# Second experts' first layer as whole products, each tile's weights by a transfer

## The reference

```python
h = einsum('btd,edh->bteh', x, W1) + b1      # D = 128, H = 512, E = 8
y = einsum('bteh,ehd->bted', gelu(h), W2) + b2
out = einsum('bted,bte->btd', y, combine)    # two experts per token, softmax weights
x = layer_norm(x + out) * gamma + beta
```

## Time and profile before

| | us |
|---|---|
| median of 3 runs (lowest, highest) | 1482.44 (1477.04, 1482.59) |
| the profiled execution | 1481.06 |
| its span | 1479.3 |
| PE busy in the span | 1286.8 (87%) |
| DVE, ACT, POOL busy | 955.5, 858.0, 606.1 |
| DMA traffic over the span | 54.68 MB, 37 GB/s |

### The profile page before, as it was taken

How to read it: one execution, slowest core, us unless ns; L and a number is a source line. 1 busy time by engine, 2 the same in 40 slices (tenths; PEclk the granted TensorE clock), 3 DMA queues, 4 the chain that set the end, 5 groups by cost and what they waited for, 6 DMA issues and landing times.

```text
span 1479.3 us, 28486 instructions
## 1 busy us (share of the span) xinstructions
PE 1286.8 (87%) x9302; PEld 793.7 (54%) x9302; DVE 955.5 (65%) x3308; ACT 858.0 (58%) x1679; POOL 606.1 (41%) x783
## 2 busy tenths in 40 slices
PE   3867899999999999999999999899888986989982
PEld 1323445555555555555555545455555654878872
DVE  4465665667576766776676766656756663676784
ACT  3775675667566766675666576645434443455553
POOL 1000233342444425342533353335435455657674
PEclk7989899999999999999999999999989998999996
DMA  8051590000000000000000000001020001142322
GB/s 333 1 214 39 9 4 1 1 9 1 8 10 14 8 1 16 8 8 1 17 7 8 1 16 1 8 5 69 2 77 16 1 8 37 46 116 70 119 74 91
DMA packets 65455, 54.68 MB, mean 37 GB/s; under 512 B 41016, under 2 KB 51648, under 8 KB 65056
## 3 DMA queue, kind: packets, MB, share of 16 engines
q1 hardware_dynamic: 60768, 43.48, 14.7%
q0 software_dynamic: 4544, 9.38, 1.9%
HBM read 21.03 MB, written 31.81 MB: 36 GB/s over the span
## 4 chain that ended last, share of the span: by engine, by line
PE 58%; DVE 22%; ACT 9%; issue 7%; POOL 2%; POOLq 1%; DMA 0%; SPq 0%; ACTq 0%; DVEq 0%
PE scores L1744 12%; PE outs L1762 9%; PE work L1684 7%; PE outs L1888 6%; DVE scores L1238 4%; DVE ra L1231 4%; PE work L1791 4%; PE scores L1875 3%; ACT ra L953 2%; ACT a_buf L947 2%; PE scores L1713 2%; PE outs L1967 2%; DVE parts L1273 2%; PE work L1850 1%; PE work L1861 1%
## 5 line engine op out<-in xcount | busy, mean ns | idle before, releaser
L1238 DVE CUSTOM_DVE_ANT_0 scores<-scores,mask_qk 128x512 f32<-128x512 f32 (+3 forms) x512 | 238.5, 517 | 168.7 <-PE scores L1713 168.6
L786 POOL TENSOR_SCALAR_AFFINE_SELECT big<-big 128x256 f32<-128x256 f32 x256 | 101.2, 408 | 496.4 <-ACT big L941 471.9
L941 ACT ACTIVATE big<-scores 128x1024 f32<-128x1024 f32 (+1 forms) x192 | 169.6, 884 | 231.6 <-PE scores L1744 231.5
L947 ACT ACTIVATE a_buf<-scores 128x1024 f32<-128x1024 f32 x256 | 248.7, 1029 | 47.2 <-PE scores L1875 47.0
L1744 PE MATMUL scores<-ra 64*128 64x512 f32 (+3 forms) x1536 | 187.6, 350 | 16.9 <-ACT a_buf L947 10.0
L806 POOL TENSOR_TENSOR big<-big 128x768 f32<-128x768 f32 x64 | 116.6, 1822 | 130.9 <-issue 52.9
L1762 PE MATMUL outs<-big 128*64 128x512 f32 (+3 forms) x1024 | 159.4, 455 | 0.0
L1744 PEld LDWEIGHTS scores<-ra 64*128 64x128 f32 x1536 | 123.4, 190 | 67.1 <-issue 45.7
L1888 PE MATMUL outs<-a_buf 128*16 128x512 f32 x1024 | 142.8, 632 | 2.0 <-ACT a_buf L947 2.0
L1022 ACT ACTIVATE big<-scores,b_sb 128x128 f32<-128x128 f32 x312 | 89.2, 369 | 76.4 <-PE scores L1955 76.4
L1231 DVE TENSOR_TENSOR ra<-work,ra 128x512 fp32r<-128x512 f32 x128 | 87.9, 687 | 69.7 <-ACT ra L953 69.4
(11 more groups left out here) (223 smaller groups left out, 2539.3 us busy)
## 6 DMA issues: line engine op xcount, KB each, us to landing
sorted_rows<-xrows SPq DMA_DIRECT2D x34, 520.0 KB, 6.7
qkT<-sorted_rows SPq DMA_DIRECT2D x78, 65.0 KB, 1.9
a_buf<-in_w SPq DMA_DIRECT2D x2, 2048.0 KB, 7.8
a_buf<-in_x SPq DMA_DIRECT2D x8, 256.0 KB, 2.7
x_rows<-x SPq DMA_DIRECT2D x8, 256.0 KB, 2.0
ra<-x_rows SPq DMA_DIRECT2D x8, 256.0 KB, 3.0
a_buf<-choice_rows SPq DMA_DIRECT2D x6, 256.0 KB, 4.0
yT<-choice_rows SPq DMA_DIRECT2D x5, 256.0 KB, 2.8
```

Source lines behind the costliest of these rows:

```text
L941: activation(prob1(g, i), d[:, :, 0:256] if i == 2 else d, ACT.Exp, scale=SCALE1).then_inc(unit_free("pair", g, i), 1)
L947: activation(prob0(c)[:, i * 1024:(i + 1) * 1024], unit_wait(act, "cosine", c, i), ACT.Exp).then_inc(unit_free("cosine", c, i), 1)
L1238: return v.tensor_tensor_reduce(scores_, scores_, mask_qk[:, SEQ - width:SEQ], -1.0, 3e38, ALU.add, ALU.min, neg_max[:, qt, j:j + 1])
```

## The change

The first layer is computed with the hidden channels on the partitions: the weight tile is the stationary operand, the transposed rows are the moving one, in four whole float32 products. Its result needs no transposing, so `hidden_moved` and `hidden_transposed` go, and so does the split of rows and weights into two float32r parts. The weights are no longer held whole: SP loads the 512 columns (256 KB) of each tile's expert into a ring of eight, behind the tile's rows. DVE copies the transposed rows (`x_T_moved`).

```diff
+W1_RING = 8
             def sorted_tile(n):
                 if n >= RING:
                     sp.wait_ge(y_tile_sent[n % RING], 16 * (n // RING))
                 at = sp.value_load(block_at[0:1, n:n + 1], min_val=0, max_val=BLOCKS - 1)
                 sp.dma_start(x_tile(n), sorted_rows[bass.ds(at * P, P), :]).then_inc(
                     x_tile_in[n % RING], 16)
+                if n >= W1_RING:
+                    sp.wait_ge(hidT_full, n - W1_RING + 1)
+                cols = sp.value_load(expert_at[0:1, n:n + 1], min_val=0,
+                                     max_val=(EXPERTS - 1) * HID1)
+                sp.dma_start(w1_tile(n), w1_1[:, bass.ds(cols, HID1)]).then_inc(
+                    w1_tile_in[n % W1_RING], 16)
...
-                if b == BATCH - 3:
-                    sp.wait_ge(x_taken, BATCH)
-                    sp.dma_start(w1_raw, w1_1).then_inc(w1_in, 16)
...
-            sp.wait_ge(sparse_ready, EXPERTS)
             for n in range(ALL_TILES):
...
-            def x_hi_part(n):                       # ACT
-                act.wait_ge(xt_full, n + 1)
-                if n >= 4:
-                    act.wait_ge(hid_full, n - 3)
-                copy(x2_hi[:, quarter(n)], xt_bank).then_inc(xt_hi, 1)
...
-                                      scores[:, n % 2, HID1 + c * P:HID1 + (c + 1) * P], ACT.Gelu,
+                                      scores[:, n % 2, c * P:(c + 1) * P], ACT.Gelu,
...
-                if o.i == BATCH - 1:
-                    act.wait_ge(w1_in, 16)
-                    copy(w1_hi[:, p * HID1:(p + 1) * HID1],
-                         w1_raw[:, p * HID1:(p + 1) * HID1]).then_inc(sparse_hi, 1)
...
-            def x_lo_part(n):                       # DVE
-                dve.wait_ge(xt_hi, n + 1)
+            def x_T_moved(n):
+                dve.wait_ge(xt_full, n + 1)
                 if n >= 4:
-                    dve.wait_ge(hid_full, n - 3)
-                v.tensor_tensor(x2_lo[:, quarter(n)], xt_bank, x2_hi[:, quarter(n)].bitcast(F32),
-                                ALU.subtract).then_inc(xt_lo, 1)
-            def hidden_moved(n):
-                dve.wait_ge(hid_full, n + 1)
-                if n >= 2:
-                    dve.wait_ge(hidT_full, n - 1)
-                v.tensor_copy(hid_rows(n), scores[:, n % 2, 0:HID1]).then_inc(hid_ready, 1)
+                    dve.wait_ge(hidT_full, n - 3)
+                v.tensor_copy(x_T(n), xt_bank).then_inc(xt_ready, 1)
...
-                if o.i == BATCH - 1:                # DVE
-                    dve.wait_ge(sparse_hi, p + 1)
-                    cols = slice(p * HID1, (p + 1) * HID1)
-                    v.tensor_tensor(w1_lo[:, cols], w1_raw[:, cols], w1_hi[:, cols].bitcast(F32),
-                                    ALU.subtract).then_inc(sparse_ready, 1)
...
             def hidden1(n):                         # PE
                 expert[n] = pe.value_load(expert_at[0:1, n:n + 1], min_val=0,
                                           max_val=(EXPERTS - 1) * HID1)
-                pe.wait_ge(xt_lo, n + 1)
-                if n >= 2:
-                    pe.wait_ge(hid_ready, n - 1)
-                d = scores[:, n % 2, 0:HID1]
-                cols = bass.ds(expert[n], HID1)
-                mm(d, x2_hi[:, quarter(n)], w1_hi[:, cols], start=True, stop=False)
-                mm(d, x2_hi[:, quarter(n)], w1_lo[:, cols], start=False, stop=False)
-                mm(d, x2_lo[:, quarter(n)], w1_hi[:, cols], start=False,
-                   stop=True).then_inc(hid_full, 1)
-            def hidden_transposed(n):
-                pe.wait_ge(hid_ready, n + 1)
+                pe.wait_ge(w1_tile_in[n % W1_RING], 16 * (n // W1_RING + 1))
+                pe.wait_ge(xt_ready, n + 1)
                 if n >= 2:
                     pe.wait_ge(hidT_ready, n - 1)
                 for c in range(CH1):
-                    last = nc.tensor.transpose(scores[:, n % 2, HID1 + c * P:HID1 + (c + 1) * P],
-                                               hid_rows(n)[:, c * P:(c + 1) * P], ident)
+                    last = mm(scores[:, n % 2, c * P:(c + 1) * P],
+                              w1_tile(n)[:, c * P:(c + 1) * P], x_T(n), start=True, stop=True)
                 last.then_inc(hidT_full, 1)
...
             def first_tiles():
-                pe.wait_ge(sparse_ready, EXPERTS)
+                pe.wait_ge(sparse_in, 16 * N_SPARSE)
```

More of the change, by code:

```diff
@@ L266 @@
 A0_BUF = XT_B + SEQ
-W1_HI = 0
-W1_LO = W1_HI + EXPERTS * HID1
-W2 = W1_LO + EXPERTS * HID1
+W1 = 0
+W2 = W1 + W1_RING * HID1
 B2 = W2 + EXPERTS * HID1
+X_T = B2 + EXPERTS * DIM
 Y_RING = 0
@@ L276 @@
 HID_AT = XB_RING + RING * DIM
-FINISH = HID_AT + 4 * HID1
+FINISH = HID_AT + 2 * HID1
 SPARSE = FINISH + EARLY.last * SEQ
@@ L427, in layers_kernel, with w1_tile @@
         tsum = big[:, TSUM:TSUM + 2 * 384].rearrange("p (j n) -> p j n", j=2)
-        w1_hi = a0_part(W1_HI, EXPERTS * HID1).bitcast(F32R)
-        w1_raw = a0_part(W1_LO, EXPERTS * HID1)
-        w1_lo = a0_part(W1_LO, EXPERTS * HID1).bitcast(F32R)
+        def w1_tile(n):
+            return a0_part(W1 + (n % W1_RING) * HID1, HID1)
         w2_1_sb = a0_part(W2, EXPERTS * HID1)
@@ L467, in xb_tile, with hid_T, x_T @@
             return ring(XB_RING, DIM, n)
-        def hid_rows(n):
+        def hid_T(n):
             return big[:, HID_AT + (n % 2) * HID1:HID_AT + (n % 2 + 1) * HID1]
-        def hid_T(n):
-            return big[:, HID_AT + (2 + n % 2) * HID1:HID_AT + (3 + n % 2) * HID1]
-        assert SPARSE <= BIG and B2 + EXPERTS * DIM <= A0_BUF
+        def x_T(n):
+            return a0_part(X_T + (n % 4) * P, P)
+        assert SPARSE <= BIG and X_T + 4 * P <= A0_BUF
         def quarter(n):
@@ L532, in layers_kernel @@
         kept = sem("kept")
-        w1_in = sem("w1_in")
         sparse_in = sem("sparse_in")
-        sparse_hi = sem("sparse_hi")
-        sparse_ready = sem("sparse_ready")
         sparse_step = sem("sparse_step")
@@ L539, in layers_kernel @@
         x_tile_in = [sem(f"x_tile_in{i}") for i in range(RING)]
+        w1_tile_in = [sem(f"w1_tile_in{i}") for i in range(W1_RING)]
         y_tile_sent = [sem(f"y_tile_sent{i}") for i in range(RING)]
         xt_full = sem("xt_full")
-        xt_hi = sem("xt_hi")
-        xt_lo = sem("xt_lo")
+        xt_ready = sem("xt_ready")
         xb_ready = sem("xb_ready")
-        hid_full = sem("hid_full")
-        hid_ready = sem("hid_ready")
         hidT_full = sem("hidT_full")
@@ L1078, in _ @@
                     act.wait_ge(tables_ready, 1)
-                    for n in range(3):
-                        x_hi_part(n)
                 if o.pair(-1) is not None:
@@ L1120, in _ @@
             for n in range(ALL_TILES):
-                if n + 3 < ALL_TILES:
-                    x_hi_part(n + 3)
                 if n == LATE.tile:
@@ L1531, in _ @@
                     for n in range(3):
-                        x_lo_part(n)
+                        x_T_moved(n)
                 if o.pair(-1) is not None:
@@ L1612, in scaled @@
                                 ALU.mult).then_inc(rows_ready["fin"], 1)
-            hidden_moved(0)
             for n in range(ALL_TILES + 1):
                 if n + 3 < ALL_TILES:
-                    x_lo_part(n + 3)
-                if n + 1 < ALL_TILES:
-                    hidden_moved(n + 1)
+                    x_T_moved(n + 3)
                 if n:
@@ L1931, in rows_transposed @@
                 if n >= 1:
-                    pe.wait_ge(xt_lo, n)
+                    pe.wait_ge(xt_ready, n)
                 nc.tensor.transpose(xt_bank, x_tile(n)[:, 0:DIM], ident).then_inc(xt_full, 1)
@@ L2104, in _ @@
                     hidden1(n + 1)
-                if n < ALL_TILES:
-                    hidden_transposed(n)
                 if n:
```

## The result

The changed kernel takes 1469.6 us (median of 5 runs, 1468.66 to 1473.0) against 1482.44 of the kernel before on the same chip: a ratio of 0.9914 (95% interval 0.9888 to 0.994), 12.8 us less. The forecast was 1450. The profiled execution took 1468.66 us, with a span of 1466.9 (before: 1481.06 and 1479.3).

A forecast was written before the change was run, and what follows sets the result against it. PE alone was taken to set the quiet pace, with DVE work causing stalls elsewhere and SP binding after tile 29. Gains 7 + 13.3 + 0 + 10.2 + 1 = 31.5 us from 1482.44 gave 1451, stated as 1450 (own range 1441 to 1458).

The forecast's parts named there:

- The start: Before the tile stage: PE no longer waits for rows and weights, its first product comes earlier; 7 us gained (5 to 11).
- the step i = 7: Step before the tile stage: eight DVE differences and as many ACT roundings go; 1 us gained (0 to 8).
- Tiles 29 to 77: Finishing stretch: SP's queue ends at 98 us, later than PE's 94, against 108.21 before; 10.2 us gained.
- SP and the transfers: SP's queue: a second table read and issue per tile make 2.22 us (2.0 to 2.5), more than PE's 1.89.
- PE's first layer ended by a DMA: Expected sign after tile 29 that SP binds: PE's first layer waits on SP's weights, issue pairs every 2.2 us.
- four tiles take it 9 us: POOL from tile 52: two added operations of about 1.2 us every fourth tile, 9 us against PE's 7.6.
- Tiles 1 to 25: First stretch of the tile stage: 24 tiles at 1.89 us plus 5 of stalls, 50.4 for 63.7; 13.3 us gained.
- I keep 5: Stalls between tiles 1 and 25: 5 of 12.3 us remain, for long routing chains and ACT's table change (0 to 12.3).
- PE stays near 2.1: Rival: PE's sequencer holds the tile near 2.1 us, only start and stalls gain; 1462 us, chance 0.09.
- dearer SP: Rival: SP costs 2.6 us per tile, adding 14 us after tile 29; about 1464 us, chance 0.15.
- SP free: Rival: SP does not bind and the lighter DVE leaves nearly no stall; about 1438 us, chance 0.17.
- Slower by blocked issues: Rival: SP's issues block while transfer engines are full, 1.15 us each, 3.03 per tile; 1490 us, chance 0.05.

The follow-up runs named there:

- the request made four tiles earlier: Changed kernel with SP issuing the finished rows' loads from tile 55 instead of tile 59: ratio 0.9865 to the kernel before.
- its repeat on the second chip: The changed kernel unaltered, run again as control on another chip: ratio 0.9919 to the kernel before.
- the ring of twelve: Changed kernel with twelve places for weight tiles instead of eight: ratio 0.9898 to the kernel before.
- the same ring with one read less: Changed kernel with twelve weight places and a fixed expert per tile, so SP makes no second table read: ratio 0.9861 to the kernel before.
- the two-bank kernel: Changed kernel with finished rows requested at tile 55 and two alternating PSUM banks for transposed rows: 1458.58 us on the third chip, 0.9852 to the kernel before.
- the version with weights by ACT: Changed kernel with two alternating PSUM banks, ACT issuing weights from tile 8 on, finished rows still requested at tile 59: 1453.64 us, 0.9831 to the kernel before.
- the resident one with two banks: Changed kernel with all weights loaded once, fixed expert per tile, two alternating PSUM banks for transposed rows: 1448.39 us, 0.9791 to the kernel before.
- moving the read: Changed kernel with finished rows requested at tile 55 and PE's table read placed ahead of the transpose: ratio 0.9864 to the kernel before.

## Why the prediction was wrong

**The mechanisms.** The rounded products and the transposes fell away and the product is as dear as the second layer (286 and 279 ns a record): right. The start: PE's first product moved from 1242.48 to 1234.84 us and tile 1's store by 8.64, against 8 forecast with the step i = 7. Tiles 25 to 29 took 16.60, forecast 16.6. SP needs 2.18 us for a pair, forecast 2.22, and an issue takes 0.33 (the longest of the weights' 78 took 0.75). The sign was right. The sum came out 19.1 us too high, in two terms.

**Tiles 29 to 77, 12.5 us of it: the gain that "is then 10.2, not 14".** The step that failed stands in "SP and the transfers", at "behind it stand the rows of n+1 and all later tiles, the residuals and finished rows". The finished rows were priced as ten issues of 0.47 us, never as a consumer with a due time. DVE needs the first of them at tile 52, in a stream on which the next tiles' copies depend. An SP that falls behind reaches its tile 59 too late, and 9 us are lost in one place (17.18 in place of 8.23). That this is the cause is shown by the request made four tiles earlier (DVE's wait 7.81 us in the changed kernel, 7.00 in its repeat on the second chip, 1.51 with the early request); that SP's pace makes it late, and not the ring of eight, is shown by the ring of twelve (8.33) against the same ring with one read less (2.57). The forecast that SP binds was thus right, but it showed where it wasn't looked for: "PE's first layer ended by a DMA" is not seen in the changed kernel, as the hole gives SP its lead back. Only where the hole is closed does PE wait for rows, 7.2 us in the two-bank kernel, and that SP's part in the weights costs it is shown by the version with weights by ACT, where those waits are gone.

With it failed the path of the sum: one end time for SP's whole queue (98) was set against one for PE and POOL (94), and the later was taken. SP's own part came out nearly right. The changed kernel's last weights leave at

```profile
1420.36 0.33 SPq L679 DMA_DIRECT2D a_buf<-in_w  x1
```

and with a landing of 2.9 that is 94.4 us behind tile 29's store, forecast 93.0. But from there to the last store it was to be 5.0 us and is 18.7. SP does not set the pace up to the last tile: it holds the tiles up once, at 52, and those behind the hole take 2.34 us each (53.88 / 23) at their own pace, while SP runs ahead. Where the hole is closed, SP's price is mis-sized as well: forecast 4 us (98 against 94); to tile 77 the two-bank kernel takes 108.7, 6.5 more than with the weights by ACT and 11.7 more than the resident one with two banks.

**The same stretch, POOL and a slip.** That "four tiles take it 9 us" was right for the kernels with two banks (9.27), and the 94 us for a stage without SP's limit were 3 low: the resident kernel with two banks takes 37.81 + 6.76 + 49.75 = 94.3 us to tile 76 and 2.6 more to tile 77. So even a free SP had less to give than the prediction said. Against that, the 98 us of the forecast ran to tile 77 and were compared with 108.21 to tile 76; like for like, 110.84 before, the forecast gain would have been 12.8, and the miss is 15.1 us and not 12.5.

**Tiles 1 to 25, 7.2 us of it: "I keep 5".** The quiet tile was 1.985 instead of 1.89, inside its bounds (1.80 to 2.0): 24 x 0.095 = 2.3. The stalls are 57.55 - 24 x 1.985 = 9.9 instead of 5: 4.9. They were tied to how much of DVE's time is free ("some 1.1 us of a 1.89 us tile"). DVE did get lighter (busy 31.33 of 57 us, before 48.44 of 67), and the stalls stayed, because about half of them are not load but order: one insertion in DVE's stream still delays the copy, one PSUM bank passes that on to PE, and PE's table read is queued behind. The two-bank kernel shows that the forecast's 5 us of stalls were attainable: 52.16 us, of which 4.5 are stalls, but by an edit that this change did not contain.

**The clock.** Before, PE was granted 2.4 GHz from 1249 us on; only the start of the stage was lower (0.59 in the earlier trace rows). Now the window 1328 to 1338 has 0.83, behind a stretch in which PE stood idle for 2.5 of 16 us; the hole itself has 0.63, and the 5 us behind it 0.56. No term had this. As an estimate from these grants, the 5 us behind the hole cost up to 2.2 and the 10 from 1328 up to 1.7; no run measures either by itself. Nor does idle time alone decide it. In the two-bank kernel on the third chip PE was no busier, and the grant stayed at 1.00 there and through tiles 49 to 53:

```profile
1316.00:1321.00 5.00, 3.18 (x25) 2.57 (x24) 0.78 (x3) 1.54 (x6) 4.20 (x5) 1.00 0.90 259
1321.00:1326.00 5.00, 3.28 (x28) 2.88 (x27) 2.13 (x6) 1.88 (x7) 4.29 (x7) 1.00 0.71 203
1326.00:1331.00 5.00, 5.00 (x46) 4.88 (x45) 1.95 (x7) 2.28 (x8) 4.33 (x7) 1.00 0.54 167
```

**The rivals.** The time lies beyond both near ones, 1462 (PE stays near 2.1) and 1464 (dearer SP), and for neither's reason: the quiet tile did shorten, and the pair cost 2.18, not 2.6. SP free: no. On that rival the Trainium skill, DMA: Bandwidth & Descriptors, Issuing engines are not separate DMA queues, calls the issue "usually small relative to the DMA itself"; the issue alone is (0.33 us beside a landing of 2.9), but with the table read that the address needs it is 1.09, and with the weights taken off SP tiles 29 to 76 were 6.5 us shorter. Slower by blocked issues: the weights' issues took 0.33, two of 78 more than 0.5.

What stays open: why every second quiet tile is 0.1 to 0.3 us longer than 1.89; the records put a gap ahead of its first layer at PE's own issue, and moving the read did not shorten it. Nor is it settled why tiles 25 to 29 take 1.5 to 2.8 us more on two of the chips. The granted clock goes with it: 0.79 to 0.91 over that stretch in all eight profiles there, 1.00 in the changed kernel's first profile. In the changed kernel's repeat on the second chip the grant at 1325 to 1331 us was 0.55, and two of POOL's stores, those of tiles 27 and 29, wait 1.29 and 1.39 us for DVE, where in the first profile no store of tiles 26 to 29 waits more than 0.17. But the resident kernel on the third chip had 0.90 over the stretch and took 16.56, and the kernel before was not profiled on the two chips.

```profile
1325.00:1331.00 6.00, 6.00 (x33) 6.00 (x32) 0.78 (x3) 1.33 (x5) 4.90 (x6) 0.55 0.62 179
1331.00:1337.00 6.00, 3.36 (x17) 3.17 (x17) 1.55 (x6) 1.93 (x8) 3.08 (x6) 0.73 0.55 161
```

## What to carry to other kernels

When a queue gets more work per turn, list everything that is issued from it, with the moment at which each consumer wants it: here the item that broke was one with little lead, not the one that was added. A stall that an insertion causes need not shrink with an engine's load; look for the buffer and the instruction order that pass it on, and price those. And where a changed register address is needed on two queues, issue from the engine that has already read it.

## What the hardware showed beside this

A transfer whose address comes from a table costs SP 1.09 us of its stream, of which the issue is 0.33; the other 0.76 are the read and what turns it into an address. With 18 MB more moved than before (73.03 MB in place of 54.68 over the span) and a DMA share of 0.56 at 179 GB/s between 1255 and 1312 us, weight tiles of 256 KB still landed in 2.9 us (median of 78, 2.6 to 4.1). And the granted clock fell to 0.83 and 0.56 in parts of the stage where the kernel before had 1.00, in the changed kernel; in the two-bank kernel on the third chip it did not.
